# Scatter-adds without a bounds check, and a row copy cut into alternate runs of 16 rows

## The reference

```
h = relu(layernorm(x))
deg = number of edges by src                      # both ends look up this one count
norm[e] = rsqrt(deg[src[e]]) * rsqrt(deg[dst[e]]) # 0 where a count is 0
msg[e] = sum_b comps[type[e], b] * (h[dst[e]] @ bases[b])      # 4 bases of 128 x 128
msg[e] = msg[e] * alpha[type[e]] * norm[e]
out = x + segment_sum(msg, src)
```

## Time and profile before

| | us |
|---|---|
| median of 3 runs | 830.52 (830.2 to 843.87) |
| the profiled execution | 832.09 |
| its span, first to last instruction | 830.0 |
| DVE busy | 595.5 (72%) |
| PE busy | 583.1 (70%) |
| POOL busy | 538.8 (65%) |
| ACT busy | 369.4 (45%) |

### The profile page before, as it was taken

One profiled execution on the slowest core, in us unless ns is written; L12 is line 12 of the kernel. 1 busy time (PEld: TensorE's weight loads), 2 busy tenths in 40 slices (PEclk: granted clock), 3 DMA queues, 4 the chain that ended last, 5 costly groups with the idle time before them and its releaser, 6 DMA issues.

```text
span 830.0 us, 13837 instructions
## 1 busy us (share of the span) xinstructions
PE 583.1 (70%) x3922; PEld 423.3 (51%) x3922; DVE 595.5 (72%) x2613; ACT 369.4 (45%) x1493; POOL 538.8 (65%) x404
## 2 busy tenths in 40 slices
PE   1219576773775887777777968858886987798760
PEld 1117474653643665545555646646664665665430
DVE  4119677775767997666787869868886897898630
ACT  0103452624254354454564545555555555555520
POOL 1208778672300577778877787788786878677775
PEclk9659878888898899899898989998999899999995
DMA  4968799899601344444444445444544353534332
GB/s 146 351 233 298 261 342 332 294 341 333 210 8 52 64 87 77 75 89 90 79 87 86 86 76 90 90 87 76 94 84 89 53 113 58 96 55 77 33 32 25
DMA packets 56527, 108.89 MB, mean 131 GB/s; under 512 B 9291, under 2 KB 48216, under 8 KB 55636
## 3 DMA queue, kind: packets, MB, share of 16 engines
q0 software_dynamic: 34496, 25.72, 23.3%
q10 hardware_dynamic: 1600, 51.20, 17.2%
q1 hardware_dynamic: 20356, 31.10, 12.4%
HBM read 94.89 MB, written 64.61 MB: 192 GB/s over the span
## 4 chain that ended last, share of the span: by engine, by line
DMA 38%; DVE 16%; issue 14%; PE 12%; POOL 11%; ACT 7%; SPq 1%; POOLq 0%; ACTq 0%; DVEq 0%
DMA out_dram<-acc,scatter_idx 17%; DMA rows<-in_x_dram,dst_i 7%; POOL out_dram L375 6%; DMA edge_row<-edge_rows 6%; DMA src_rows<-rows 5%; POOL rows L355 4%; PE pst L714 4%; DVE masked L462 4%; PE pst L733 3%; DVE turned_hot L456 3%; DVE part_sum L497 3%; ACT scratch L591 3%; PE pst L700 2%; DMA rows<-edge_rows 2%; ACT scratch L583 2%
## 5 line engine op out<-in xcount | busy, mean ns | idle before, releaser
L375 POOL DMA_INDIRECT out_dram<-acc,scatter_idx x196 | 312.2, 1593 | 139.5 <-ACT acc L638 61.3
L355 POOL DMA_INDIRECT rows<-in_x_dram,dst_i x196 | 224.6, 1146 | 144.0 <-PE pst L700 56.0
L714 PE MATMUL pst<-table_bits,turned_hot 128*128 128x198 f16 x1568 | 183.9, 266 | 78.5 <-DVE masked L462 74.7
L733 PE MATMUL pst<-bases_sb,h_turned 128*128 128x512 f32 x392 | 217.9, 639 | 0.0
L714 PEld LDWEIGHTS pst<-table_bits,turned_hot 128*128 128x128 f16 x1568 | 149.5, 106 | 103.9 <-issue 55.9
L497 DVE SCALAR_TENSOR_TENSOR part_sum<-pst,coef,part_sum 128x128 f32<-128x128 f32 x392 | 115.4, 344 | 105.2 <-ACT part_sum L628 104.6
L741 PEld LDWEIGHTS pst<-rows,same 128*128 128x128 f32 x392 | 75.3, 206 | 184.4 <-issue 153.4
L462 DVE SCALAR_TENSOR_TENSOR masked<-iota_h,lo,pst 128x198 f32<-128x198 f16 x392 | 141.2, 415 | 7.1 <-PE pst L714 7.0
L741 PE MATMUL pst<-rows,same 128*128 128x128 f32 x392 | 86.5, 305 | 69.4 <-ACT acc L638 63.5
L628 ACT ACTIVATE part_sum<-pst,coef 128x128 f32<-128x128 f32 x196 | 71.0, 362 | 135.3 <-PE pst L733 134.0
L583 ACT ACTIVATE scratch<-rows 128x128 f32<-128x128 f32 x196 | 57.8, 297 | 157.8 <-DMA rows<-in_x_dram,dst_i 157.8
(11 more groups left out here) (71 smaller groups left out, 410.4 us busy)
## 6 DMA issues: line engine op xcount, KB each, us to landing
out_dram<-in_x_dram ACTq DMA_DIRECT2D x50, 1000.0 KB
src_row<-src_rows SPq DMA_DIRECT2D x27, 512.0 KB, 3.9
edge_row<-edge_rows SPq DMA_DIRECT2D x49, 256.0 KB, 4.9
rows<-in_x_dram,dst_i POOLq DMA_INDIRECT x196, 4.6
out_dram<-acc,scatter_idx POOLq DMA_INDIRECT x196
rows<-edge_rows SPq DMA_DIRECT2D x14, 175.0 KB
src_row<-src_rows SPq DMA_DIRECT2D x1, 448.0 KB, 3.7
out_dram<-in_x_dram SPq DMA_DIRECT2D x1, 304.0 KB, 3.3
```

The source lines that it names most:

```text
L355: pool.indirect_dma_start(row(t), None, x, bass.IndirectOffsetOnAxis(ap=dst_i[:, t:t + 1], axis=0)) \
L375: pool.indirect_dma_start(out, bass.IndirectOffsetOnAxis(ap=scatter_idx[:, t:t + 1], axis=0), acc[:, t % ACC_RING, :], None, bounds_check= ...
L714: last = pe.matmul(pst[:, LOOK + t % 2, k * LO:(k + 1) * LO], turned_hot[:, g % 2, c, k * W + j * P:k * W + (j + 1) * P], table[:, c * LO: ...
L733: pe.matmul(pst[:, PRODUCT + t % 4, :], h_turned[:, g % 2, j, :], bases_sb[:].rearrange("d b f -> d (b f)"), start=True, stop=True).then_i ...
```

## The change

The scatter's `bounds_check` and `oob_is_err` go. The copy still has 50 pieces of 1.024 MB. A pair of pieces now covers 4000 rows, cut into 250 runs of 16 rows (8,192 B); the first piece of the pair takes the 125 even runs, the second the 125 odd ones. Two pieces in place of eight are issued ahead of the first group, and three in place of two ahead of each `stats`, both before and within the main loop, until all 50 are issued.

```diff
     COPIES = 50
-    COPY_ROWS = N // COPIES
-    COPIES_FIRST = 8
+    COPY_RUN = 16
+    COPY_ROWS = 2 * N // COPIES
+    COPIES_FIRST, COPIES_EACH = 2, 3
...
                 pool.indirect_dma_start(out, bass.IndirectOffsetOnAxis(ap=scatter_idx[:, t:t + 1], axis=0),
-                                        acc[:, t % ACC_RING, :], None, bounds_check=out.shape[0] - 1,
-                                        oob_is_err=True, compute_op=ALU.add).then_inc(scattered[t % 2], 16)
+                                        acc[:, t % ACC_RING, :], None, compute_op=ALU.add) \
+                    .then_inc(scattered[t % 2], 16)
...
             def copy():
                 if copy_at[0] < COPIES:
-                    a = copy_at[0] * COPY_ROWS
+                    a = copy_at[0] // 2 * COPY_ROWS
+                    odd = copy_at[0] % 2
                     copy_at[0] += 1
-                    flat_out, flat_x = (y[a:a + COPY_ROWS, :].rearrange("r d -> (r d)") for y in (out, x))
-                    act.dma_start(flat_out.rearrange("(q e) -> q e", q=32), flat_x.rearrange("(q e) -> q e", q=32)) \
-                        .then_inc(copied, 16)
+                    runs_out, runs_x = (y[a:a + COPY_ROWS, :].rearrange("(q r) d -> q (r d)", r=COPY_RUN)[odd::2, :]
+                                        for y in (out, x))
+                    act.dma_start(runs_out, runs_x).then_inc(copied, 16)
...
-                copy()
-                copy()
+                for _ in range(COPIES_EACH):
+                    copy()
                 stats(g)
```

More of the change, by code:

```diff
@@ L98, in build @@
     COPIES = 50
-    COPY_ROWS = N // COPIES
-    COPIES_FIRST = 8
-    assert COPIES * COPY_ROWS == N
+    COPY_RUN = 16
+    COPY_ROWS = 2 * N // COPIES
+    COPIES_FIRST, COPIES_EACH = 2, 3
+    assert COPIES // 2 * COPY_ROWS == N and COPY_ROWS % (2 * COPY_RUN) in (0, COPY_RUN)
     rows16_dram = nc.dram_tensor("edge_rows", (3, TILES * P), F16, kind="Internal").ap()
```

## The result

The changed kernel takes 1033.2 us, the kernel before 830.4 us on the same chip: the ratio is 1.245, with a 95% interval of 1.242 to 1.249. The profiled execution took 1034.1 us, its span is 1032.0 us. The lines of the copy and the scatters have moved by 2 to 4: the gathers are L357, the scatters L377, the copy L580.

What follows compares the result with a forecast made beforehand. The prediction took a 270.7 us front, covering the copy, and a 559.3 us POOL-paced scatter phase as the bounds. With the copy now ending at 453: 453 + 559.3 - 5 - 53 = 954, plus 0.5, 955 us; range 885 to 1050.

Steps and rivals of the forecast that it cites:

- the check worth nothing: Rival, scatters: copy on five engines, but dropping the bounds check saves nothing; 1007 us, chance 0.19.
- ACT's hold: Rival: ACT stands at its copy issues when its queue is full; up to 63 us, 955 to 1017, chance 0.09.
- Five engines: Copy: 125 runs have 5 as largest divisor up to 16, so each piece runs on 5 DMA engines.
- The copy's end: Copy's last landing: 13 + 410 + 30 = 453 us, between 423 and 509.
- the two prices: Copy: rate of one DMA engine, 22.4 or 25 GB/s, giving 410 to 457 us; 410 was taken.
- The queue doesn't run dry: ACT's copy queue: three more pieces, some 25 us of work for five engines, follow with each stats group.
- The check at 0.27 us each, 53 us: Scatters: dropping the bounds check saves 0.27 us on each of 196, 53 us in all, bounds 0 to 90.
- the prediction's own sign: Scatter's median duration: if it stays at 1.57 us, the 53 us of saving fall out.
- POOL paces the scatter phase: Scatter phase, 559.3 us: POOL sets the pace, taken up for 284 of 300 us in the steady stretch.
- Ready `acc` tiles, 5 us: Start of the scatter phase: six tiles ready after the copy save POOL 5 us of waits, at most 12.
- The front's gain is covered: Front: fewer pieces at once remove most of SP's 40.5 us store wait, worth nothing under the longer copy.
- the sixteen-engine rival: Rival: copy stays on 16 engines and hidden, front loses 30 us, scatters 53; 747 us, 700 to 800, chance 0.12.

Runs made afterwards that it cites:

- each2: The changed kernel with two copy pieces instead of three issued ahead of each stats: 991.4 us, ratio 1.183.
- no_check: The kernel before with only the bounds check taken off the scatters: 822.2 us, ratio 0.987.
- copy_only: The changed kernel with the bounds check put back on the scatters: 1048.5 us, ratio 1.258.
- blocks_new_order: The changed kernel with the old copy pieces (one block of 2000 rows, packets of 64,000 B) in the new issue order, no check: 822.9 us, ratio 0.986.
- runs126: The changed kernel with 126 runs in each copy piece instead of 125, the last two pieces plain blocks: 801.1 us, ratio 0.960.
- run80: The changed kernel with copy runs of 80 rows instead of 16, so 25 runs in a piece: 1030.9 us, ratio 1.237.

## Why the prediction was right, and where not

The forecast was 955 us, the range 885 to 1050, and 1033.2 lies in it. That five engines do the copy and the copy becomes the bound was right in kind and decided the direction. That the time lies within the range is partly luck: none of the cases gives it alone (the check worth nothing ends at 1007, ACT's hold at 1017), and the range reaches so far above 955 for a slower copy, which didn't come, together with a check worth nothing. By its steps:

- **Five engines, 0.88 for all such cases together**: right, 250 reports.
- **The copy's end**: 453 us forecast, 441 measured (share 0.44 in the 41 us up to there, 0.10 behind it). 10.24 MB in 428 us with all that runs beside it, 26.3 GB/s while a packet is moved; of the two prices, 22.4 and 25 GB/s, the faster was the right end, and still a little low.
- **"The queue doesn't run dry", and ACT's hold as a rival with 0.09**: the queue didn't run dry, but it was full. I had put its price at nothing if seven pieces fit, and at up to 63 us; four fit, and the first scatter came 49 us behind the copy. `each2` shows these 49 us to be the hold's, so the rival should have been in the main sum. Its count was off too: a piece is 25 + 1 packets for each of the five engines, not 50. The row that I should have pressed was the one with 50 x 2 packets for each engine: no more than 18 of them were ever in the queue at the end of an issue, and the change put 1,300 through each of five.
- **The check at 0.27 us each, 53 us**: wrong in place and size. The duration didn't change, and by the prediction's own sign the 53 us fall out; 10 to 20 us came from between the instructions, and not at every scatter. That is nearer to the rival in which it is worth nothing.
- **POOL paces the scatter phase**: the step that failed in kind. That POOL was in use or in its 0.30 us gaps for 284 of 300 us was true, but DVE's 83 and PE's 80 of 100 us weren't slack of 17%: with 117 us taken off POOL the phase gave back 15 us, 3%. A check of 0.27 us could hardly have given 53 us where 0.6 us gave 15. The prediction had named the sign: a phase after the copy that isn't near 500 us. It was 542.
- **Ready `acc` tiles, 5 us**: `no_check` and the changed kernel differ by 3.6 us in the phase, `copy_only` and before by nothing; small, as said.
- **The front's gain is covered**: right. SP's wait fell to 15.1 us with nothing to show for it. But the 30 us that the sixteen-engine rival gave the front for it aren't borne out: `blocks_new_order` has a wait of 19.3 us and a front of 273.9 us. The front became shorter with the smaller packets on fourteen or sixteen engines (256.3 and 265.7 us), and more with the later order (242.3).

The sum: 955 - 12 (copy) + 49 (hold) + 41 (the phase to the end of the span, 542 us and not 501) = 1033. Two errors on the same side; the copy's end made up for a quarter of one.

## What to carry to other kernels

Ahead of reshaping a DMA issued from ACT or SP, factor its outermost count: 97 got one engine here, 125 and 25 got five, and the number of small packets on the queue says how many worked. An engine that issues DMAs is held once its queue is full, and everything written behind the issue in its stream is held with it, so issue late pieces behind the work that the next phase needs. An engine whose gaps are all closed isn't yet the bound: take its work away in one run and see how far the phase follows.

## What the hardware showed that I had not expected

- ACT's issue of a DMA lasts as long as its queue has no room: 0.6 us with short queues, up to 19.6 us here. The room isn't a fixed number of pieces: at the end of a held issue 87 to 102 packets were left for each of five engines with 25 + 1 to a piece, 71 to 78 with 5 + 1, and 55 to 72 for each of fourteen with 9 + 1 (`runs126`).
- A packet's length in one queue is another queue's delay: edge-row loads of 256 KB took 59.4 us beside packets of 40,960 B and 10.8 us beside 8,192 B, on five shared engines; SP's wait for its stores was 44.3 us in `run80` and 15.1 in the changed kernel.
- How fast an engine moves the copy's packets went with the number of engines at work more than with the packets' size: 26.3 GB/s with five (8,192 B), 26.1 with ten (10,240 B), 24.8 with fourteen (8,192 B), 22.0 with sixteen (12,800 B) and 22.4 with sixteen (64,000 B).
- An indirect scatter with addition holds POOL 0.6 us longer than one without (1572 against 974 ns). A bounds check lengthens neither the instruction nor the usual gap of 0.30 us ahead of it; it made 53 to 66 gaps of 195 longer than that, where 29 to 36 were without it.
